# Two sets of banks and buffers, or three, in the expert stage of a two-layer network

## What is computed

```python
def _L1_ffn_ref(x, router_w, bias, shared_w_gate, shared_w_up, shared_w_down, w_gate, w_up, w_down):
    ...
    hg = jnp.einsum('ecd,efd->ecf', expert_in, w_gate)
    hu = jnp.einsum('ecd,efd->ecf', expert_in, w_up)
    expert_out = jnp.einsum('ecf,edf->ecd', jax.nn.silu(hg) * hu, w_down)
    ...
    return shared_out + sparse.reshape(B, S, D)
```

## Time and profile before

| what | value |
|---|---|
| time, median of 3 runs (lowest to highest) | 1695.61 us (1694.96 to 1705.65) |
| the profiled execution | 1696.94 us, of it span 1695.1 us |
| first `up` of block 0 | 1247.9 us into the span |
| copy of bank 6 (L961), blocks 0 to 5 | 1342.97, 1412.79, 1482.15, 1551.53, 1620.89, 1690.06 us |

### The profile page before, as it was taken

One profiled execution on the slowest core, in us unless ns is written; L12 is line 12 of the kernel. 1 busy time (PEld: TensorE's weight loads), 2 busy tenths in 40 slices (PEclk: granted clock), 3 DMA queues, 4 the chain that ended last, 5 costly groups with the idle time before them and its releaser, 6 DMA issues. The chain is left out here.

```text
span 1695.1 us, 34204 instructions
## 1 busy us (share of the span) xinstructions
PE 1550.0 (91%) x11598; PEld 1000.8 (59%) x11598; DVE 1053.0 (62%) x2087; ACT 724.8 (43%) x1269; POOL 559.7 (33%) x603
## 2 busy tenths in 40 slices
PE   2889999999997799999999999999987899999998
PEld 1556666666664467777777777778853333333333
DVE  4754445444345977777767677754657666666665
ACT  2231122122222146555545554566656455555554
POOL 2110001001006635203430344005954455555554
PEclk6999999999998899999999999999999999999999
DMA  7320110100004626203330333001222243343433
GB/s 195 104 87 22 30 30 10 35 25 14 1 1 108 166 65 127 65 15 76 94 83 6 73 92 88 6 19 36 82 85 88 90 129 113 115 122 112 124 113 92
DMA packets 142627, 124.45 MB, mean 73 GB/s; under 512 B 86613, under 2 KB 123949, under 8 KB 141485
## 3 DMA queue, kind: packets, MB, share of 16 engines
q1 hardware_dynamic: 127053, 110.62, 24.2%
q0 software_dynamic: 1152, 8.39, 1.6%
q10 hardware_dynamic: 14304, 3.81, 1.1%
HBM read 102.54 MB, written 5.28 MB: 64 GB/s over the span
## 5 line engine op out<-in xcount | busy, mean ns | idle before, releaser
L1187 DVE TENSOR_REDUCE region_c<-ps 120x1 f32<-120x512 f32 x336 | 225.5, 688 | 109.7 <-PE ps L1610 106.4
L870 ACT ACTIVATE region_c<-ps 128x720 f16<-128x720 f32 (+1 forms) x228 | 175.3, 769 | 274.9 <-PE ps L1640 274.9
L737 POOL TENSOR_TENSOR region_c<-region_c 128x480 f16<-128x480 f32 x198 | 216.9, 1096 | 221.9 <-ACT region_c L957 221.9
L1180 DVE TENSOR_TENSOR region_c<-ps,region_c 128x720 f16<-128x720 f32 (+1 forms) x228 | 206.1, 904 | 90.9 <-ACT ps L871 87.1
L1510 PE MATMUL ps<-region_k 128*128 128x360 f16 (+1 forms) x752 | 239.6, 319 | 5.2 <-ACT m L849 5.2
L1512 PE MATMUL ps<-region_k 128*128 128x360 f16 (+1 forms) x752 | 239.0, 318 | 0.0
L1511 PE MATMUL ps<-region_k 128*128 128x360 f16 (+1 forms) x752 | 238.7, 317 | 0.0
L657 POOL TENSOR_TENSOR vare<-mv,eps 120x6 f32<-120x6 f32 x20 | 4.0, 198 | 629.9 <-DVE mv L1112 629.9
L1657 PE MATMUL ps<-region_k,region_c 128*120 128x129 f16 (+1 forms) x1368 | 179.9, 221 | 0.0
L1658 PE MATMUL ps<-region_k,region_c 128*120 128x128 f16 (+1 forms) x1368 | 179.2, 220 | 0.0
L951 ACT ACTIVATE region_c<-ps 128x480 f32<-128x480 f32 x198 | 112.3, 570 | 153.8 <-PE ps L1736 123.2
(11 more groups left out here) (233 smaller groups left out, 2749.3 us busy)
## 6 DMA issues: line engine op xcount, KB each, us to landing
gates<-gates_dram SPq DMA_DIRECT2D x288, 120.0 KB, 2.7
region_c<-in_k SPq DMA_DIRECT2D x56, 256.0 KB, 2.7
region_c<-in_v SPq DMA_DIRECT2D x56, 256.0 KB, 3.0
region_k<-gates_dram SPq DMA_DIRECT2D x96, 120.0 KB, 2.8
region_c<-in_WcT POOLq DMA_DIRECT2D x8, 1024.0 KB, 5.9
region_c<-in_experts SPq DMA_DIRECT2D x18, 352.0 KB, 2.9
gates<-band_dram SPq DMA_DIRECT2D x26, 189.0 KB
region_k<-region_c SPq DMA_TRANSPOSE x120, 2.8
```

Source lines behind the costliest of these rows:

```text
L737: g.tensor_tensor(a_lo[u], ac[u], a_hi[u], ALU.subtract).then_inc(s["a_lo_ready"], 1)
L870: a.activation(halves(p_hi[u][0:parts]), st, ACT.Exp).then_inc(s["p_hi_ready"], 1)
L1180: v.tensor_tensor(halves(p_lo[u][0:parts]), two(2 * u, parts), halves(p_hi[u][0:parts]), ALU.subtract).then_inc(s["lo_ready"], 1)
L1187: v.tensor_reduce(mxk[:, r, bass.ds(c + 1, 1)], bank(bk, P), AX, ALU.max).then_inc(s["mx_free"], 1)
```

## The change

Everything that existed twice exists three times, step n uses set n % 3, and gt has three buffers instead of four. The banks of set u are 2u and 2u+1 instead of 3u and 3u+1. TensorE runs `up(n+3)` and then `down(n)`. The inner loops have three steps a body on all four engines; 33 steps are 11 bodies of three, of which TensorE, ScalarE and VectorE take the first, and TensorE the last too, out of the loop. At a block's start the three last `down`s of the block before stand between the three first `up`s, and the turn comes behind the fourth `up`. The transfers of the gates wait for L1357 of step n-3 (gated_ready), those of a block's first three pairs for the last L1357 of the block before. sg, a_hi, a_lo, out_cm and fin lie in another region of SBUF.

```diff
-        ac = [region_c.take(MT) for _ in range(2)]
+        ac = [region_c.take(MT) for _ in range(SETS)]
...
-        gt = [gates32[:, n * MT:(n + 1) * MT] for n in range(3)] + [region_k.take(MT)]
+        gt = [gates32[:, n * MT:(n + 1) * MT] for n in range(SETS)]
...
+            def spread(c, n):
...
+                if n > SETS:
+                    sp.wait_ge(s["gated_ready"], PAIRS * c + n - SETS)
+                elif not isinstance(c, int):
+                    sp.wait_ge(s["gated_ready"], PAIRS * c)
...
-            for u in range(4):
-                spread(0, 0, u)
-            with sp.Fori(1, PAIRS // 4) as p4:
-                for u in range(4):
-                    sp.wait_ge(s["a_ready"], 4 * p4 + u - 2)
-                    spread(0, p4, u)
+            for n in range(1, NSEQ):
+                spread(0, n)
...
-                            ("up_free", 2), ("down_done", 2), ("fin_out", 16)):
+                            ("up_free", SETS), ("down_done", SETS), ("fin_out", 16)):
...
             with act.Fori(1, NMC) as c:
                 n0 = NSEQ * c
-                silu(n0, 0)
-                with act.Fori(0, PAIRS // 2) as i:
-                    silu(n0 + 2 * i + 1, 1)
-                    high_part(n0 + 2 * i, 0)
-                    silu(n0 + 2 * i + 2, 0)
-                    high_part(n0 + 2 * i + 1, 1)
-                high_part(n0 + PAIRS, 0)
+                for n in range(SETS):
+                    silu(n0 + n, n)
+                    if n:
+                        high_part(n0 + n - 1, n - 1)
+                with act.Fori(1, NSEQ // SETS) as i:
+                    for u in range(SETS):
+                        silu(n0 + SETS * i + u, u)
+                        high_part(n0 + SETS * i + (u - 1), (u - 1) % SETS)
+                high_part(n0 + PAIRS, PAIRS % SETS)
                 chunk_done(c)
...
                 shared_product(n0)
+                for n in range(1, SETS):
+                    product(n0 + n, n, PAIRS * c + n, GATED[n] * c + 1)
                 chunk_done(c - 1)
-                with dve.Fori(0, PAIRS // 4) as i:
-                    for k in range(4):
-                        m = 4 * i + k + 1
-                        product(n0 + m, (k + 1) % 2, PAIRS * c + m, PAIRS // 4 * c + i, k)
+                with dve.Fori(1, NSEQ // SETS) as i:
+                    for u in range(SETS):
+                        m = SETS * i + u
+                        product(n0 + m, u, PAIRS * c + m, GATED[u] * c + i + (u > 0))
...
             for n in range(NSEQ):
-                if n + 2 < NSEQ:
-                    up(0, n + 2, n % 2, n + 2)
-                if n + 1 < NSEQ:
-                    down(n, n % 2, n, start=(n == 0))
+                if n + SETS < NSEQ:
+                    up(0, n + SETS, n % SETS, n + SETS)
+                    down(n, n % SETS, n, start=(n == 0))
...
-                pe.wait_ge(s["up_free"], n0 + 2)
-                up(c, 0, 0, n0)
-                down(PAIRS, 0, n0 - 1, stop=True)
-                up(c, 1, 1, n0 + 1)
+                for n in range(SETS):
+                    up(c, n, n, n0 + n)
+                    down(NSEQ - SETS + n, n, n0 + (n - SETS), stop=(n == SETS - 1))
+                up(c, SETS, 0, n0 + SETS)
                 chunk_done(c - 1)
-                up(c, 2, 0, n0 + 2)
                 down(0, 0, n0, start=True)
-                with pe.Fori(0, PAIRS // 2 - 1) as i:
-                    up(c, 2 * i + 3, 1, n0 + 2 * i + 3)
-                    down(2 * i + 1, 1, n0 + 2 * i + 1)
-                    up(c, 2 * i + 4, 0, n0 + 2 * i + 4)
-                    down(2 * i + 2, 0, n0 + 2 * i + 2)
-                down(PAIRS - 1, 1, n0 + PAIRS - 1)
-            down(PAIRS, 0, NSEQ * NMC - 1, stop=True)
+                with pe.Fori(1, NSEQ // SETS - 1) as i:
+                    for u in (1, 2, 3):
+                        up(c, SETS * i + u, u % SETS, n0 + SETS * i + u)
+                        down(SETS * i + (u - SETS), u % SETS, n0 + SETS * i + (u - SETS))
+                for n in range(NSEQ - 2, NSEQ):
+                    up(c, n, n % SETS, n0 + n)
+                    down(n - SETS, n % SETS, n0 + (n - SETS))
+            for n in range(NSEQ - SETS, NSEQ):
+                down(n, n % SETS, NSEQ * (NMC - 1) + n, stop=(n == NSEQ - 1))
             chunk_done(NMC - 1)
```

More of the change, by code:

```diff
@@ L53 @@
 NMC = B * T // MT
+SETS = 3
+GATED = [len([n for n in range(1, NSEQ) if n % SETS == u]) for u in range(SETS)]
 EPS = 1e-5
@@ L404, in tower @@
         region_c.at = 0
-        ac = [region_c.take(MT) for _ in range(2)]
-        out_cm = region_c.take(MT)
+        ac = [region_c.take(MT) for _ in range(SETS)]
         assert region_c.at <= 2 * T
[L408 to L412, removed]
-        region_k.at = KSET
-        gt = [gates32[:, n * MT:(n + 1) * MT] for n in range(3)] + [region_k.take(MT)]
+        region_k.at = KSET
+        out_cm = region_k.take(MT)
+        sg = [region_k.take(MT) for _ in range(SETS)]
+        a_hi = [region_k.take(MT, dtype=F16) for _ in range(SETS)]
+        a_lo = [region_k.take(MT, dtype=F16) for _ in range(SETS)]
+        fin = region_k.take(MT // P, C)[0:P]
+        gt = [gates32[:, n * MT:(n + 1) * MT] for n in range(SETS)]
         gates_dram = nc.dram_tensor("gates_dram", [E, B * T], F32).ap()
@@ L439, in tower @@
         s_tail = sem("tail_in")
-        s_gt = [sem(f"gates_in{u}") for u in range(4)]
+        s_gt = [sem(f"gates_in{u}") for u in range(SETS)]
         s_vt = [sem(f"v_turned{u}") for u in range(2)]
@@ L739, in _ @@
             for n in range(NSEQ):
-                low_part(n, n % 2)
+                low_part(n, n % SETS)
                 for k in range(2):
@@ L744, in _ @@
             with pool.Fori(1, NMC) as c:
-                low_part(NSEQ * c, 0)
-                with pool.Fori(0, PAIRS // 2) as i:
-                    low_part(NSEQ * c + 2 * i + 1, 1)
-                    low_part(NSEQ * c + 2 * i + 2, 0)
+                with pool.Fori(0, NSEQ // SETS) as i:
+                    for u in range(SETS):
+                        low_part(NSEQ * c + SETS * i + u, u)
         @block.scalar
@@ L967, in _ @@
                 if n + 1 < NSEQ:
-                    silu(n + 1, (n + 1) % 2)
-                high_part(n, n % 2)
+                    silu(n + 1, (n + 1) % SETS)
+                high_part(n, n % SETS)
                 for x in beside(B, "act", pair=n):
@@ L1350, in _, with product @@
             stage_end(dve, 1)
-            def product(n, u, m, turn, k):
-                gated = bank(3 * u + 1)[:, 0:MT]
+            def product(n, u, m, turn):
+                gated = bank(2 * u + 1)[:, 0:MT]
                 dve.wait_ge(s["up_ps"], n + 1)
-                dve.wait_ge(s_gt[k], 32 * turn + 32)
-                v.scalar_tensor_tensor(out=gated, in0=gated, scalar=A_SCALE / X_SCALE ** 2, in1=gt[k],
+                dve.wait_ge(s_gt[u], 32 * turn)
+                v.scalar_tensor_tensor(out=gated, in0=gated, scalar=A_SCALE / X_SCALE ** 2, in1=gt[u],
                                        op0=ALU.mult, op1=ALU.mult).then_inc(s["gated_ready"], 1)
@@ L1386, in _ @@
             for n in range(1, NSEQ):
-                product(n, n % 2, n, (n - 1) // 4, (n - 1) % 4)
+                product(n, n % SETS, n, n // SETS + (n % SETS > 0))
                 for x in beside(B, "dve", pair=n):
```

31 lines of the change are left out of this document (14 added, 17 removed).

## The result

The changed kernel takes 1677.69 us, the median of 4 runs (1674.08 to 1679.17), beside 1696.64 us of the kernel before on the same chip (4 runs, 1694.96 to 1705.65). The ratio is 0.9875, with a 95% interval of 0.9842 to 0.9908. I had predicted 1687.5 us, range 1679 to 1698, with 0.79 on a change within 1%.

The account below looks back on a forecast made before the run. TensorE was taken to bound the kernel before, VectorE after. Five blocks' 7.2 us plus 1 us of block 0, off the profiled 1696.94, gave 1688.7; the runs' median lies 1.3 lower, hence 1687.5 us, range 1679 to 1698.

Parts of the forecast that it names:

- The order of the argument: In the loops: VectorE has 0.56 us slack in 8.06; the third set moves the bound from TensorE to VectorE.
- The stall at the block's start: TensorE stands 2.04 us ahead of a block's fourth `up`, which needs set 0.
- forecast place: VectorE at a block's start: shared product ends at 2.12 us, product 1 at 3.94, product 2 at 5.65.
- The gates: Gate transfers with three buffers: 3.6 to 4.2 us needed, 5.2 available, no cost; coming late as a rival, chance 0.03.
- The block's end: After VectorE's loop, the last `down` starts at 2.09 us and its last matmul at 2.50, ending a 68.0 us block.
- the same formula: VectorE's loop in a block: 30 products, 9 edges and two kinds of gap, 10 each, sum to 58.0 us.
- 9 x 1.02: VectorE's inner loop: nine edges a block, each standing 1.02 us as in the old loop.
- 10 x 0.47: VectorE's inner loop: ten gaps a block of 0.47 us, ahead of the second product with one more register row.
- The extra register row: In VectorE's second product: 0.11 us, the difference of idle times 0.47 and 0.36; nothing if it hides.
- a longer edge as a rival: VectorE's loop edges lengthen: 0.1 us more each costs 4.5 us, 1712 us at 1.58 us an edge; chance 0.08.
- the first rival: TensorE stays the bound, VectorE's edge partly hidden: blocks of 65.5 us, 1675.5 us in all; chance 0.14.
- Block 0: The first block, without loops: at best 4.4 us less waiting of VectorE, 1 us taken.

Follow-up runs that it names:

- the two medians: Changed kernel with 242 and with 243 increments of an unused semaphore on VectorE ahead of its loop over blocks: 1709.41 and 1699.32 us.

## Why the prediction failed

**What held.** The order of the argument stood. VectorE's loop had little slack before; its edge was covered then; with the third set TensorE waits at most once in a body of three steps, and the bound moves to VectorE. The stall at the block's start was 2.04 us as worked out, and each product came within 0.07 us of its forecast place. The gates never came late in the changed kernel. The block's end was right in sum: with the measured idle times put into the same formula, the loop takes 30 x 1.35 + 9 x 0.75 + 10 x 0.37 + 10 x 0.41 = 55.05 us instead of 58.0, 2.95 less, and 68.0 - 2.95 = 65.05 us is the 65.03 measured. That it fits to 0.02 us is partly luck: the loop begins 0.17 us earlier than forecast (7.35 us after the last matmul, not 7.52) and lasts 55.17 us by the trace of block 3.

**What failed** is the term "9 x 1.02" and, beside it, "10 x 0.47". The edge in the changed loop is 0.75 us, nine of them 2.4 us less a block: 1.9 by the place of the head and the rest by less register work. The extra register row costs 0.04 us beyond the ordinary gap, not 0.11, ten of them 0.6 us less. That is 3.0 us a block and 15 us in five, where the five blocks came out 339.9 - 325.7 = 14.2 us below the forecast. I wrote of the edge that "the rows are of this very loop, so the sum goes by them". They were rows of the old loop at its old place, and the new one had other instructions at its head and another address. The 0.66 us that I put on the edge beyond an ordinary gap were themselves 0.44 of the edge proper and 0.22 of the boundary. With its loop across the boundary as before, the changed kernel has blocks of 66.8 us and would take, by an estimate from the two medians, some 1677.7 + 10.1 = 1687.8 us. The forecast would then have looked right by luck, with 1.2 us a block still too much in it.

The Trainium skill (Advanced Engine Details and Errata, Control Flow Timing) gives a compare-and-branch as about 108 ns; I had set that aside as the price of an edge, and rightly. In the trace of the changed kernel the instruction itself lasts 0.050 to 0.074 us, and the whole edge costs 0.75 - 0.37 = 0.38 us more than an ordinary gap at its best place. With 0.11 in its stead TensorE would have been the bound, and the written-out loops speak against that.

**The range.** I had priced a longer edge as a rival and the register row at nothing for the lower end, but a shorter edge only within the rival in which TensorE takes over. The bound "below, the ordinary gap of 0.36" was missing: it would have put the loop at 30 x 1.35 + 19 x 0.36 + 10 x 0.47 = 52.0 us, with TensorE the bound, and the low end of the range at the first rival's time (1675.5 us as I gave it; by its own terms its five blocks are 19.7 us less, not 19, and its time 1674.9).

**Block 0** gave nothing (forecast 1 us). Where its granted clock was 0.98 it took 95.0 to 95.1 us with two sets and, in one run, 95.4 with three; where it was 0.93 to 0.96 it took 96.1 to 97.1 us with either (the kernels with the silus first left out). Most of the 1.9 us more in the first comparison goes with that clock (0.98 in the earlier trace rows, 0.95 after).

## What to carry over

When a change moves the bound from one engine to another, the new bound's gaps that were covered so far become terms of the sum. They have never been tested at their old size, so each needs a range down to the ordinary gap and up. A near time doesn't prove a mechanism: writing out one engine's loop at a time shows in two runs which engine bounds. And where a short loop is the bound, see where its instructions lie, or write it out.

## What the runs showed of the hardware

VectorE's taken branch is followed by a gap of 0.14 us, or of 0.23 to 0.24 us (0.26 to 0.29 the first time) if it goes back over a boundary in its stream. Two such boundaries showed, ahead of instructions 2218 and 2474; whether one lies halfway is open. Passing one forward costs another 0.10 to 0.14 us where nothing covers it, and took 0.36 us the first time, between two increments. For a body of three products the two together were 0.21 us of 5.6, and 10.1 us of the kernel. A fused row of register work lasts 0.107 us for 3 operations and 0.151 to 0.154 for 5, and at the head of VectorE's loop here nothing hides it. An increment of a semaphore takes VectorE 0.09 us.
